# Binary FFN weights laid out transposed by the host, and the gate and up weights of a chunk split in one piece

## The reference

```python
xn = layernorm(x)
s = nf4_attention_and_ffn(xn)      # weights from 4-bit codes, with LoRA; the second half of the kernel
def binary_diff_weight(w, base):   # for w1 (gate), w3 (up), w2 (down)
    d = w - base
    return base + mean(abs(d)) * sign(d)
gate = einsum('bsh,ih->bsi', xn, W1)       # W1, W3: [1792, 512]
up   = einsum('bsh,ih->bsi', xn, W3)
ffn  = einsum('bsi,hi->bsh', silu(gate) * up, W2)   # W2: [512, 1792]
return x + s * silu(ffn)
```

## Time and profile before

| what | value |
|---|---|
| median of 3 runs | 632.92 us (630.64 to 638.28) |
| profiled execution, from its first to its last instruction | 632.0 us |
| PE busy | 584.8 us, 93% |
| DVE busy | 487.1 us, 77% |
| ACT busy | 348.1 us, 55% |
| POOL busy | 157.4 us, 25% |
| moved from and to HBM | 63.09 MB |

### The profile page before, as it was taken

How to read it: one execution, slowest core, us unless ns; L and a number is a source line. 1 busy time by engine, 2 the same in 40 slices (tenths; PEclk the granted TensorE clock), 3 DMA queues, 4 the chain that set the end, 5 groups by cost and what they waited for, 6 DMA issues and landing times.

```text
span 632.0 us, 8467 instructions
## 1 busy us (share of the span) xinstructions
PE 584.8 (93%) x2794; PEld 480.9 (76%) x2794; DVE 487.1 (77%) x569; ACT 348.1 (55%) x447; POOL 157.4 (25%) x110
## 2 busy tenths in 40 slices
PE   0698799998999899999999899999999999999993
PEld 0577678886878788888678688888888888888883
DVE  5956776498999999889674488887878888887347
ACT  2547562464655537576443585776848577583210
POOL 3413206543343452210120011011111011111005
PEclk9989899998999999999999999999999999999998
DMA  8798748324333331100730011020111101100303
GB/s 339 305 398 304 200 135 239 114 97 165 100 128 95 95 114 50 51 1 5 158 134 1 0 52 51 11 65 24 50 50 50 50 0 50 50 0 15 118 1 133
DMA packets 56964, 63.09 MB, mean 100 GB/s; under 512 B 15216, under 2 KB 36720, under 8 KB 56944
## 3 DMA queue, kind: packets, MB, share of 16 engines
q1 hardware_dynamic: 56944, 62.84, 30.4%
HBM read 60.73 MB, written 2.10 MB: 99 GB/s over the span
## 4 chain that ended last, share of the span: by engine, by line
PE 71%; DVE 12%; issue 7%; ACT 5%; DMA 2%; POOL 2%; SPq 1%; POOLq 0%; DVEq 0%; ACTq 0%
PE gate_ps L1416 16%; PE up_ps L1416 16%; PE sum_ps L1437 10%; PE tr_ps L1294 5%; PE up_ps L1437 4%; PE gate_ps L1437 4%; PE sum_ps L1590 4%; PE up_ps L1335 3%; DVE weight L1000 3%; PE tr_ps L1398 2%; DVE attn_sum L1040 1%; PE gate_ps L1346 1%; DVE y L923 1%; DMA y<-L_attn_x 1%; ACT ramp L668 1%
## 5 line engine op out<-in xcount | busy, mean ns | idle before, releaser
L1416 PE MATMUL up_ps<-xT,guT 128*128 128x512 f32 x576 | 138.4, 393 | 0.0
L1416 PE MATMUL gate_ps<-xT,guT 128*128 128x512 f32 x576 | 138.4, 393 | 0.0
L1031 DVE SCALAR_TENSOR_TENSOR base<-ramp,base 128x1536 f32<-128x1536 f32 x70 | 122.6, 1752 | 3.6 <-ACT ramp L658 2.1
L1416 PEld LDWEIGHTS up_ps<-xT,guT 128*128 128x128 f32 x576 | 107.0, 188 | 21.5
L1416 PEld LDWEIGHTS gate_ps<-xT,guT 128*128 128x128 f32 x576 | 107.0, 188 | 21.5
L658 ACT ACTIVATE ramp<-raw,ramp_bias 128x1536 f32<-128x1536 int32 x70 | 108.9, 1577 | 0.0
L440 POOL TENSOR_TENSOR weight<-base,scale_trio 128x1536 f32<-128x1536 f32 x14 | 38.7, 2767 | 244.6 <-DVE base L1031 244.6
L1437 PE MATMUL sum_ps<-downT,h_split 128*128 128x512 f32 x288 | 72.1, 400 | 5.1 <-DVE h_split L1021 5.1
L1437 PEld LDWEIGHTS sum_ps<-downT,h_split 128*128 128x128 f32 x288 | 54.3, 192 | 17.3 <-issue 6.4
L627 ACT ACTIVATE guT<-tr_ps 128x512 fp32r<-128x512 f32 x48 | 28.7, 597 | 64.8 <-PE tr_ps L1398 37.2
L639 ACT ACTIVATE h_split<-up_ps 128x512 fp32r<-128x512 f32 x48 | 28.7, 598 | 64.6 <-DVE up_ps L1014 64.6
(11 more groups left out here) (192 smaller groups left out, 798.7 us busy)
## 6 DMA issues: line engine op xcount, KB each, us to landing
raw<-L_ffn_w SPq DMA_DIRECT2D x42, 256.0 KB, 3.6
base<-L_ffn_mean_w SPq DMA_DIRECT2D x42, 256.0 KB, 4.9
scan<-L_ffn_w SPq DMA_DIRECT2D x12, 640.0 KB, 7.8
scan<-L_ffn_mean_w SPq DMA_DIRECT2D x12, 640.0 KB, 8.9
raw<-L_attn_codes_gu SPq DMA_DIRECT2D x14, 512.0 KB, 3.7
attn_codes<-L_attn_codes_attn SPq DMA_DIRECT2D x4, 1024.0 KB, 4.7
raw<-L_attn_codes_down SPq DMA_DIRECT2D x14, 256.0 KB, 3.9
y<-L_attn_x SPq DMA_DIRECT2D x2, 1024.0 KB, 6.5
```

Of the source, the lines that this page charges most:

```text
L1031: nc.vector.scalar_tensor_tensor(base[:, par, :], ramp[:, (step % 2) * TRIO:(step % 2 + 1) * TRIO], NF4_RAMPS[j][2], base[:, par, :], ALU. ...
L1416: last = nc.tensor.matmul(ps, guT[:, par, kind, w_part, hc * P:(hc + 1) * P], xT[:, x_part, hc, th * HALF:(th + 1) * HALF], start=(hc == 0 ...
```

## The change

The host now builds two arrays, `w_laid` and `mean_laid`, each [3, 128, 14 x 512]: for every unit, the transposed 128 x 512 block that PE used to make, with 2 KB in a row for each partition. The kernel loads units as they are needed by the matmuls, makes `weight` as before, and takes the high and low parts from `weight` in SBUF. All transposes of block 0's weights are gone (41 units and the eight early pieces); waits on `tr_done` become waits on `ffn_weight`, `w_lo`, `gate_done`, `up_done` and `down_done`. For chunks 4 to 13, gate and up of a chunk are split by one ACT and one DVE instruction of 1024 columns (`w_high_both`, `w_low_both`). The sums over all weights read the same amount from the new arrays.

```diff
-    scan_v = [m[FIRST * P:, :].rearrange("(p a) n -> p (a n)", p=P).rearrange("p (k s) -> p k s", s=SCAN)
-              for m in (w1, mean_w1, w3, mean_w3)] + [m[:, :, FIRST * P:] for m in (w2_v, mean_w2_v)]
+    scan_v = [m[kind, :, FIRST * HID:].rearrange("p (k s) -> p k s", s=SCAN)
+              for kind in range(3) for m in (w_laid, mean_laid)]
...
             def load_ffn(c, par):
                 sp.wait_ge(ffn_weight, 3 * c - 3)
-                for dst, gate, up, down in ((raw, w1, w3, w2_v), (base, mean_w1, mean_w3, mean_w2_v)):
-                    sp.dma_start(dst[:, par, 0:HID], gate[ds(c * P, P), :]).then_inc(chunk_loaded[par], 16)
-                    sp.dma_start(dst[:, par, HID:2 * HID], up[ds(c * P, P), :]).then_inc(chunk_loaded[par], 16)
-                    sp.dma_start(dst[:, par, 2 * HID:].rearrange("p (q i) -> p q i", q=HC),
-                                 down[:, :, ds(c * P, P)]).then_inc(chunk_loaded[par], 16)
+                for dst, src in ((raw, w_laid), (base, mean_laid)):
+                    for kind in (GATE, UP, DOWN):
+                        sp.dma_start(dst[:, par, kind * HID:(kind + 1) * HID], src[kind, :, ds(c * HID, HID)]
+                                     ).then_inc(chunk_loaded[par], 16)
...
             def early_high():
-                act.wait_ge(tr_done, 1)
-                nc.scalar.activation(signT[:, :], sum_ps[:, 1, :], ACT.Copy).then_inc(sign_T, 1)
-                nc.scalar.activation(first_w(0)[:, HI, :], sum_ps[:, 0, :], ACT.Copy).then_inc(w_hi, 1)
+                nc.scalar.activation(signT[:, :], raw_s[:, 0, :], ACT.Sign).then_inc(sign_T, 1)
+                act.wait_ge(first_loaded[0], 32)
+                nc.scalar.activation(first_w(0)[:, HI, :], base_s[:, 0, :], ACT.Copy).then_inc(w_hi, 1)
...
+            def w_high_both(c, par):
+                act.wait_ge(ffn_weight, 3 * c + UP + 1)
+                act.wait_ge(gate_done, 2 * c - 2)
+                act.wait_ge(up_done, 2 * c - 2)
+                nc.scalar.activation(guT[:, par, :, HI, :],
+                                     weight[:, par, 0:2 * HID].rearrange("p (m h) -> p m h", m=2), ACT.Copy
+                                     ).then_inc(w_hi, 2)
...
             def w_low(block_no, c, par, kind):
                 dve.wait_ge(w_hi, unit_index(block_no, c, kind) + 1)
                 buf = downT[:, par] if kind == DOWN else guT[:, par, kind]
-                nc.vector.tensor_tensor(buf[:, LO, :], tr_ps[:, (3 * par + kind) % 2, :],
+                src = weight[:, par, kind * HID:(kind + 1) * HID] if block_no == 0 else tr_ps[:, (3 * par + kind) % 2, :]
+                nc.vector.tensor_tensor(buf[:, LO, :], src,
                                         buf[:, HI, :].bitcast(f32), ALU.subtract).then_inc(w_lo, 1)
+            def w_low_both(c, par):
+                dve.wait_ge(w_hi, unit_index(0, c, UP) + 1)
+                nc.vector.tensor_tensor(guT[:, par, :, LO, :],
+                                        weight[:, par, 0:2 * HID].rearrange("p (m h) -> p m h", m=2),
+                                        guT[:, par, :, HI, :].bitcast(f32), ALU.subtract).then_inc(w_lo, 2)
...
             def ffn_make(c, par, kind):
-                dve.wait_ge(sign_ready, FIRST_UNITS + c - FIRST + 1)
-                dve.wait_ge(tr_done, 3 * c - 3)
+                dve.wait_ge(sign_ready, FIRST_UNITS + c - FIRST)
+                dve.wait_ge(w_lo, 3 * c - 3)
...
             def unit(block_no, c, par, kind):
+                if block_no == 0:
+                    return
...
+    def project_tiles(w):
+        return w.reshape(CHUNKS, P, HC, P).transpose(3, 0, 2, 1).reshape(P, CHUNKS * HID)
+    def down_tiles(w):
+        return w.T.reshape(CHUNKS, P, HID).transpose(1, 0, 2).reshape(P, CHUNKS * HID)
+    def laid(gate, up, down):
+        return np.stack([project_tiles(gate), project_tiles(up), down_tiles(down)])
```

144 lines of the change are left out of this document (63 added, 81 removed).

## The result

The changed kernel takes 647.2 us in the median of four runs (645.7 to 647.6); the kernel before took 633.1 beside it. The recorded ratio is 1.0195, with a 95% interval of 1.0139 to 1.0252; it is an estimate of its own and not the quotient of the two medians, which is 1.022. Forecast were 635.4 us and a range of 625 to 641, so the prediction is wrong, by 12 us and on the slow side. The profiled execution has a span of 645.7 us against 632.0: 13.7 us to be explained.

The account below looks back on a forecast made before the run. It took a DVE chain with POOL's holds to bound iterations 2 to 4, with PE having room. Terms -1.0 + 3.9 + 0 - 0.9 + 0 + 0.5 = +2.5 on 632.0 gave 634.5, median 635.4 us; range 625 to 641.

Parts of the forecast that it names:

- Rival 1: Whole kernel: PE is the bound after all and all removed units come out, giving 611 us; chance 0.08.
- the signs: Expected marks: PE busy about 22 us less, 3 to 5 us waits before down(0), low parts of 2 to 4 us.
- The start: Up to the first downs: unit 0's low part -0.4, PE's units -0.1, earlier loads -0.5; together -1.0 us (-3 to 0).
- Iterations 2 to 4: POOL holds low parts that now read SBUF: +1.3 us a turn, three times, +3.9 us (-4.5 to +6.9).
- a load that lands at M + 7.9: Iterations 2 to 4, no load gain; M ends an iteration's first makes; w_low goes first, a turn costs 2.3 us.
- I expect six transfers to land about 1.3 us earlier: Chunk loads in the iterations: longer DOWN rows bring landing to 6.6 us after the first makes, instead of 7.9.
- Iterations 5 and 6: Iteration 5: 0 up to down(0), then -0.9 us from two units fewer; iteration 6: 0 (-1.5 to +0.5).
- The clock: PE's granted clock falls after longer waits; hidden by DVE in iterations 2 to 4, after 5 +0.5 us (0 to 3).
- Rival 3: Waits before down(0) lower the clock in all five iterations, downs 1.5 to 2.9 us longer, 647 us; chance 0.05.
- Rival 2: Low parts slip past POOL unheld, turns of iterations 2 to 4 1.5 us shorter, 625.7 us; chance 0.27.
- The joined instruction: DVE's two low parts joined into one of 1024 columns: gain 0 to 0.1 us per chunk, taken as 0.

Follow-up runs that it names:

- e12: Changed kernel with POOL's large work in the first block's iterations taken away (subtraction of 8 columns, scalings replaced by a one-element copy); 617.9 us.
- e13: Kernel before with the same large POOL work taken away as in e12; 625.5 us.
- e10: Changed kernel with only the start's low parts (units 1 to 11) subtracting from a stale PSUM bank; 643.8 us.
- e19: Kernel before with the chunk subtraction moved from POOL to DVE and the first attention-weight step to ScalarE; 628.0 us.
- e2: Kernel before with the change's host layout and loads alone, PE still transposing and low parts reading PSUM; 633.3 us.
- e3: Changed kernel with POOL's subtraction of a chunk in three instructions of 512 columns instead of one of 1536; 645.0 us.
- e9: Changed kernel with POOL's subtractions (chunk 4's, and one per iteration) waiting until DVE's low parts are done; 643.5 us.
- e11: Changed kernel with DVE's low part of DOWN b moved behind the halves of h, and POOL waiting with chunk 4 as in e9; 643.1 us.
- e6: Changed kernel with the first block's low parts (but the very first) subtracting from a stale PSUM bank, still without PE transposes; 633.1 us.
- e4: Changed kernel with idle identity transposes filling PE's waits ahead of the first block's downs and second chunks' UP projections; 643.2 us.
- e7: e6 with the idle PE transposes of e4 added; 636.9 us.
- e5: Changed kernel with gate and up split apart again in 512 columns each, low parts still reading SBUF; 646.5 us.
- e14: Changed kernel with down weights (chunks from 4 on, start's last two) made straight into two PSUM banks and split from there; 636.0 us.
- e18: e14 with POOL's chunk subtraction in the iterations given to DVE and the first attention-weight step to ScalarE; 625.7 us.

## Why the prediction was wrong

**What bounds the kernel: right.** The turn of iterations 2 to 4 is a DVE chain with POOL's holds in it, and PE's 22 us are not on it. Rival 1 (611 us) fell. e12 against e13 shows what PE's units are worth once POOL is out of the way. Of the signs, PE's waits ahead of down(0) (3.25, 3.24 and 4.76 us) and low parts of 3.8 to 3.9 us came as written; PE's busy time fell by 8.6 us instead of 22, and POOL's subtraction didn't come earlier.

**The start, "Together -1.0": the step that failed most.** It came out at +4.2 us at M2, 5.2 us off. "From there to the first downs, DVE and ACT set the pace ... -0.1" went by the pace and left out what the prediction itself says of low parts: they now read two SBUF inputs, here too. I looked for POOL's holds in the iterations and at unit 0 and not at units 10 and 11, over which POOL's subtraction of chunk 4 already lay (94.70 and 94.11 in the rows above). The hold cost 3.0 us (4.24 instead of 1.28), the slow first downs behind it 1.3 + 0.9 us (2.90 and 2.43 for six). The first downs of e10, with only the start's low parts back in PSUM, and of e19, whose start is that of the kernel before:
```profile
94.73 1.62 PE L1367 MATMUL sum_ps<-downT,h_split 128*128 128x512 f32 x6 [1.30 <-DVE downT_more L978]
```
```profile
94.40 1.58 PE L1385 MATMUL sum_ps<-downT,h_split 128*128 128x512 f32 x6
```
e10 starts them 3.3 us ahead of the changed kernel and 1.4 ahead of the trace of the kernel before, but 0.3 behind e19. So the hold is shown, and what PE's eleven units are worth here, which I put at 0.1, isn't.

**Iterations 2 to 4, "+3.9": right in sign and place, mis-sized.** The three turns grew by 5.7 us, 1.9 each: 0.7 in the mean up to the second makes and 1.2 behind them. The term had 2.3 for a load that lands at M + 7.9 and 1.9 for 6.6; I took 1.3, between 6.0 and 6.6. The transfers landed at M + 7.6, 7.5 and 8.1. DVE came to the low part of DOWN b at M + 7.7 each time, so that POOL was ahead by 0.1 to 0.2 us in iterations 2 and 3 and behind in iteration 4; "at 7.9, w_low goes first" hung on that little. The failed step is "I expect six transfers to land about 1.3 us earlier": I had carried the times of one NF4 transfer each over to three pairs of 256 KB, of which a third got longer rows. The Trainium skill (DMA: Bandwidth & Descriptors, Specifications), by which 512 bytes are enough for line rate, had spoken against that step; e2 agrees with it to a few tenths of a us, and I had overruled it.
There is a second flaw beneath the size. The working followed one held low part and what queued behind it, as if a turn could be mended by moving it. e3, e9 and e11 move or split it, and the three turns stay at 119.9 to 121.3 us.

**Iterations 5 and 6, "0" and "-0.9".** The downs of 5 without their two units are 0.85 us shorter (267.09 to 278.11 against 257.38 to 269.25): right. Iteration 6 was 3.0 us longer where I said "0", with "POOL's scaling, which now holds w_low DOWN b" named and priced at nothing. Without that hold the 0 comes true: from the start of the iteration to down(0) it is 23.7 us in the kernel before and 23.9 in e6, whose PE waits 1.93 us in place of the four units. In the changed kernel w_low DOWN b takes 1.81 us, PE waits 2.51, and it is 25.0, which makes 1.2; and the first group of downs takes 4.58 instead of 2.88 us (3.01 in e6), which makes 1.7.

**The clock, "+0.5".** In the turns nothing, as said: "DVE hides it". In e6 the slow first group didn't lengthen them. Outside of the turns it was more: 2.2 us in the first downs and 1.7 in iteration 6, both behind waits that the holds had lengthened. Another 0.9 stand at the second block's first projections (3.80 instead of 2.89 us for twelve), and these aren't the holds' doing: the wait ahead is the same 1.8 us in the kernel before, and e6 has the slow group too (3.76).

**The rivals.** Rival 3 has the right number, 647 us, by luck: the granted clock fell after the waits, as it says, but e4, e6 and e7 show that this isn't what the turns are made of. Rival 2 (the low parts slip past) happened once: in iteration 4 the low part came at 216.72, ahead of POOL at 217.10, and took 0.69 us; that turn grew by 2.0 us all the same, 0.3 of it up to the second makes and 1.7 behind them.

**The joined instruction, "I take 0": right** (e5).

**The rule behind it.** Rows 4 and 5 had shown both halves: DVE's work on two SBUF inputs stands still beside POOL, work from PSUM doesn't. The Trainium skill (SBUF — State Buffer, Who interferes with whom) says the same, and also that the order of issue decides who blocks, not the kind of operation. e9 and e11 agree: 6.6 and 6.2 us for low part and makes, whichever comes first. What I didn't draw from it is that the pair of engines is one resource here: a turn should be costed by the sum of DVE's two-input time and POOL's, and the change adds six low parts (3.6 us of spacing) to it, of which 1.9 came through. That sum was not measured for a whole turn; P rests on e9, e11 and e12 against e13.

## What to carry to other kernels

Where DVE and GpSimd share a stage, count DVE's work on two SBUF inputs and GpSimd's work on SBUF as one engine's; here, moving a held instruction only moved the wait. An operand in PSUM can be worth keeping for that alone: transposing through PSUM had let DVE's low parts run beside POOL, and writing the make's result into a free bank (e14) gives that back for the down weights, at no cost that shows. When a change alters where an operand lives, look at every place that uses it, not only at the one that the profile has already made interesting.

## What the runs showed of the hardware

- DVE's scalar_tensor_tensor of 512 columns from two SBUF inputs takes 0.75 us into PSUM as into SBUF (e18).
- Subtracting 1536 columns takes POOL 3.5 us (kernel before); DVE did the same in 1.75 to 2.16 (e18).
- The hold goes both ways: POOL's product for w_o of 512 columns takes 1.04 us in the kernel before and 2.03 in the changed one, where it starts at 201.25 us, within DVE's low part of 200.41 + 1.96.
- After 20 transposes and then 1.58 us of rest, 3.8 us behind the last projection, the next twelve matmuls take 3.01 us at a granted clock of 1.00, that is 2.4 GHz (e4); after 3.25 us of rest alone twelve took 4.60 (changed kernel). Rests of about 2 us went either way: 2.09 us and then 4.54, 2.14 us and then 3.03 (kernel before). The Trainium skill (TensorE: Matmul & The Clock Gate, Part 4: PE-mode transpose) says that a transpose doesn't count as PE being busy in the same way; e4 doesn't bear that out.
